# A two-layer block on eight cores: a recurrent scan, token by token, replaced by two sweeps over 32 segments, with gate and routing of the expert layer rewritten

## The chip, the cores and the metric

One Trainium2 chip, all eight NeuronCores, each with its own sequence; nothing is exchanged. The metric is the device time in microseconds (us) of the slowest core. Engines: TensorE (PE; PEld is its weight load), VectorE (DVE), ScalarE (ACT), GpSimd (POOL) and SyncE (SP). SP and POOL issue the DMAs.

## The reference

Per sequence x is 2048 tokens by 1024. What the change touches is layer 0:

```python
def step(state, inp):                      # L0_attn: 128 states
    u_t, sp_t = inp                        # u = x Wi^T + bi, sp = x Ws^T + bs
    state = jnp.tanh(state @ A.T + u_t @ B.T) + sp_t
    y_t = state @ C.T
    return (state, y_t)
...
out = jnp.einsum('bsn,dn->bsd', ys, Wo) + bo
...
x = _layernorm(x + _L0_attn_ref(...))
# L0_ffn: 8 experts of 1024 -> 4096 -> 1024, the best 2 by softmax(x gate_w^T + gate_b)
x = _layernorm(x + _L0_ffn_ref(...))
```

Layer 1 is causal attention of 16 heads with a norm of k and q per head, and a channel mix with a sigmoid gate; both again with residual and layer norm. All inputs and the output are f32.

## The kernel before, in words

The program is recorded by small helpers (`E`, and `DV`, `AC`, `GP`, `MM`, `DMA` for one engine each) into one list per engine, and `realize` writes the lists out; each engine executes its own in order. So the order of the calls is the order on every engine, and nearly every instruction has the same line, L1173; the products of the scan have L1167 (`held_`), the gathers L1158. `w=` names what an instruction waits for. `only_if(flag, tok, name)` puts a block behind a branch that every engine takes or skips after it has waited for `tok`; there is one for an expert with more than CAP = 640 tokens ("x") and two for large layer norm weights ("z", "zz").

*Scan.* A state is tanh + sp, so with C_t = u_t B^T + sp_(t-1) A^T made ahead for 512 tokens in a PSUM bank (`sp_mm`, `sp_ev`, `c_mm`, BWi being Wi and B in one matrix), a token is one product of A with the tanh of the token before, added into its PSUM column, and one tanh of that column:

```python
    for t in range(T):
        if t > 0:
            hold("AT", AT)
            held(ps[:, (t // 512) % 2, t % 512:t % 512 + 1], AT, tanh[:, t - 1:t], (("ac", t),), "sc_p")
...
        E("scalar", "activation", tanh[:, t:t + 1], ps[:, (t // 512) % 2, t % 512:t % 512 + 1], AF.Tanh,
          w=w, s="ac")
        for f in sched.pop(t, ()):
            f()
```

The dictionary `sched`, filled by `at(t, f)`, hangs all other work on a token number: a tile of 128 tokens follows the scan that far behind. Per tile: `tile_state` (stb = tanh + sp), `tile_mm` (stb times WoC, which is C and Wo in one matrix), `tile_xb` (x + bo on POOL), `tile_ln` (residual and layer norm, x1 to DRAM, x1b in bf16), `tile_logit` (eight 1024-wide multiply-and-sum on VectorE, one per expert, with gwr, the gate's rows spread over all partitions), `tile_route` (the best two as one-hot rows, with ties to the lower number), `tile_rank_mm` and `tile_pos` (the row of each token in its expert's list, posU, from running counts) and two indirect DMAs that scatter x1b into xgs. `center` takes the mean off 16 blocks of Wq and Wk and stores them in wcs. W1 of expert 0 is loaded in 16 chunks during the scan, and SP fills xgs with zeros in ten DMAs.

*After the scan.* The overflow flag and the gate values; on SP `load_b2(0)` and `load_xg(0)`, the transposed load of expert 0's rows; on POOL 16 chunks of W2; the branch "x"; then `mlp` for each of eight experts: 512 products of 320 columns (hT = relu(W1 x + b1)) and 320 of 512 columns (yst, to ybs), while POOL loads the next expert's chunks, each 1 MB of f32 in DRAM that lands as 512 KB of bf16, as soon as a chunk's last reader is done. Then the x1 tiles are fetched, the two expert rows of each token gathered with posU and weighted with `gate` (`fetch`, `combine`), and attention and the last block follow.

Of the kernel before, what the change touches and what calls it, by code (L numbers as in the profile page):

```python
# [13 lines left out]
T = 2048  # L14
# [9 lines left out]
LIM = 40.0  # L24

# [4 lines left out]
def build():  # L30
# [9 lines left out]
    xT_d = din("xT", [D, T])  # L40
# [3 lines left out]
    gw_d = din("gw", [NE, D])  # L44
    cf_d = din("cf", [128, 310])
    cb_d = din("cb", [128, 640], BF16)
# [16 lines left out]
    ao_d = scratch("aos", [8, 128, T], BF16)  # L63

# [15 lines left out]
    b2r = [place(f"b2r{i}", [128, D], F32, OB + i * 4096) for i in range(2)]  # L80
# [4 lines left out]
    ohs = [place(f"oh{i}", [128, NTILE, NE], BF16, OM + 2560 + i * 256) for i in range(2)]  # L85
    posU = place("posU", [128, NTILE, 2], U32, OM + 3072)
    MX = place("MX", [128, NTILE], F32, OM + 3200)
    gate = [place(f"gate{i}", [128, NTILE], F32, OM + 3264 + i * 64) for i in range(2)]
    Mcum = [place(f"Mcum{i}", [128, NE], BF16, OM + 3392 + i * 32) for i in range(2)]
    Mt = [place(f"Mt{i}", [128, NE], BF16, OM + 3456 + i * 32) for i in range(2)]  # L90
    flag = place("flag", [128, 2], U32, OM + 3520)
# [11 lines left out]
    xTb = [place(f"xTb{i}", [128, 8, 512], BF16, O2 + i * 8192) for i in range(2)]  # L103
    gwr = place("gwr", [128, NE, D], F32, O2 + 16384)
    bor = place("bor", [128, D], F32, O2 + 49152)
    WoC = place("WoC", [128, D], BF16, O2 + 53248)
    BWi = place("BWi", [128, 8, 128], BF16, O2 + 55296)
    WsB = place("WsB", [128, 8, 128], BF16, O2 + 57344)
    WiN = place("WiN", [128, D], BF16, O2 + 59392)
    WoB = place("WoB", [128, D], BF16, O2 + 61440)  # L110
    AT = place("AT", [128, 128], BF16, O2 + 63488)
    BT = place("BT", [128, 128], BF16, O2 + 63744)
    CN = place("CN", [128, 128], BF16, O2 + 64000)
    bib = place("bib", [128, 512], BF16, O2 + 64256)

    spf = place("spf", [128, T], F32, OH)
    tanh = place("tanh", [128, T], BF16, OH + 8192)
    spb = place("spb", [128, T], BF16, OH + 12288)
    stb = place("stb", [128, T], BF16, OH + 16384)
# [108 lines left out]


    DMA("sync", "lc", cf, cf_d)  # L230
    DMA("sync", "lc", cb, cb_d[:, 0:384])
    t_lc = V("lc")
    DMA("gpsimd", "lw", WiN, WiN_d)
    DMA("gpsimd", "lw", BT, BT_d)
# [78 lines left out]
    for k in range(10):  # L313
        c_mm(0, k)()
# [950 lines left out]
```

How the kernel before makes its waits and increments, by code:

```python
    def run(eng, lst):  # L1144
        for method, args, kw, need, s, n in lst:
            plain = method in HELD or method in ("wait_", "if_", "gather_")
            for sn, v in need if plain else need[:-1]:
                eng.wait_ge(sems[sn], v)
            if method == "wait_":
                continue
            if method == "gather_":
# [4 lines left out]
                        for c in calls:  # L1156
                            call = {k: v for k, v in c.items() if k != "sem"}
                            eng.indirect_dma_start(**call).then_inc(sems[c["sem"][0]], 16)
                continue
# [5 lines left out]
            if method == "held_":  # L1165
                out, weights, rhs = args
                ins = eng.add_instruction(mybir.InstMatmult(
                    name=nc.get_next_instruction_name(), engine=mybir.EngineType.PE, start_tensor_calc=False,
                    stop_tensor_calc=True, tile_size=(128, 128), tile_position=(0, 0), ldweights=False,
                    bass_skip_group_check=True, ins=(eng.lower_ap(rhs), eng.lower_ap(weights)),
                    outs=(eng.lower_ap(out),)))
            else:
                ins = getattr(eng, method)(*args, **kw)
            if need and not plain:
                ins._wait_ge(sems[need[-1][0]], need[-1][1])
            if s is not None:
                ins.then_inc(sems[s], n)
```

## Time and profile before

| | |
|---|---|
| median of 3 runs | 3124.77 us (3118.58 to 3244.63) |
| the profiled execution | 3126.89 us |
| its span, slowest core (core 2) | 3125.2 us |
| spans of the eight cores | 3100.1 to 3125.2 us |
| mean granted TensorE clock | 0.813 |
| busy: PE, PEld, DVE, ACT, POOL | 2225.8, 974.8, 904.7, 1106.0, 480.9 us |
| HBM read, written | 371.72 MB, 69.34 MB |

Busy time is that of one profiled execution; a product's end is modelled, so start-to-start times say more of TensorE than the durations do. "Idle before" of a group is the time its engine stood still just before its instructions, with what ended it. A DMA's time is that from issue to landing. GB/s counts the bytes as they are written: the W chunks are read with twice as many. The clock is the share of 2.4 GHz granted to TensorE.

### The profile page before, as it was taken

The numbers are of one execution on the slowest core, as the hardware profiler recorded it, in microseconds if no ns is written. First come the engines' busy times: TensorE is split into PE (matmuls) and PEld (weight loads), VectorE is DVE, ScalarE is ACT, GpSimd is POOL, SyncE is SP. The second block draws the span as 40 slices with busy tenths as digits, with TensorE's granted clock in tenths as the row PEclk, the third lists the DMA queues.
The fourth block names the chain that finished last, engine by engine and source line by source line (L and its number), as shares of the span: only waits on it lengthen the run. The fifth ranks groups of instructions, "written<-read, shape, count | busy, mean of one in ns | idle before, by whom it ended". The sixth has DMA issues, their size and how long they took to land.

```text
span 3125.2 us, 29218 instructions; the slowest of 8 cores (3100.1 to 3125.2 us)
## 1 busy us (share of the span) xinstructions
PE 2225.8 (71%) x12243; PEld 974.8 (31%) x10294; DVE 904.7 (29%) x1758; ACT 1106.0 (35%) x3045; POOL 480.9 (15%) x503
## 2 busy tenths in 40 slices
PE   2434334333336999999999999956787878848775
PEld 0000000000004564656556465622332323323332
DVE  1334353434432000000000000016643444444454
ACT  1444444444432120302112030204576877823322
POOL 1011010111002021110101011013102323202223
PEclk7555555555557999999999999988998999979888
DMA  9322331111107997979799797536400123151101
GB/s 211 92 69 72 74 78 41 51 41 50 42 24 135 163 166 141 171 141 171 143 159 151 143 169 143 96 122 230 153 8 1 28 44 59 29 117 44 49 27 41
DMA packets 133009, 303.98 MB, mean 97 GB/s; under 512 B 56049, under 2 KB 60530, under 8 KB 130546
## 3 DMA queue, kind: packets, MB, share of 16 engines
q0 software_dynamic: 55152, 174.97, 32.2%
q1 hardware_dynamic: 77698, 126.96, 14.3%
q8 instruction: 92, 1.51, 0.2%
q14 instruction: 67, 0.55, 0.1%
HBM read 371.72 MB, written 69.34 MB: 141 GB/s over the span
## 4 chain that ended last, share of the span: by engine, by line
PE 56%; ACT 20%; issue 11%; DVE 7%; DMA 4%; POOL 3%; POOLq 0%; ACTq 0%; DVEq 0%; SPq 0%
PE ps L1173 45%; ACT tanh L1173 11%; PE ps L1167 11%; ACT PT L1173 4%; ACT rsd L1173 2%; DVE PT L1173 2%; DMA xTb<-xT 2%; POOL x3f L1173 1%; DVE lstf L1173 1%; DVE xk L1173 1%; ACT sq L1173 1%; DMA sumC<-stg 1%; DVE rf L1173 1%; DVE lsmf L1173 1%; POOL yB L1158 1%
## 5 line engine op out<-in xcount | busy, mean ns | idle before, releaser
L1167 PE MATMUL ps<-tanh,AT 128*128 128x1 bf16 x2047 | 336.2, 164 | 513.2 <-ACT tanh L1173 513.1
L1173 PE MATMUL ps<-xgT,W 128*128 128x320 bf16 x4096 | 560.0, 300 | 14.7 <-DMA xgT<-xgs 14.6
L1173 ACT ACTIVATE tanh<-ps 128x1 bf16<-128x1 f32 x2048 | 355.2, 173 | 573.1 <-PE ps L1167 548.6
L1173 PE MATMUL ps<-W,hT 128*128 128x512 bf16 x2560 | 553.8, 379 | 0.0
L1173 ACT ACTIVATE hT<-ps,cf 128x640 bf16<-128x640 f32 x256 | 203.3, 794 | 834.0 <-PE ps L1173 834.0
L1173 PEld LDWEIGHTS ps<-xgT,W 128*128 128x128 bf16 x4096 | 401.4, 98 | 173.0 <-issue 14.7
L1173 DVE TENSOR_TENSOR yst<-ps,b2r 128x1024 f32<-128x1024 f32 x40 | 49.0, 1225 | 1074.7 <-PE ps L1173 1060.2
L1173 PEld LDWEIGHTS ps<-W,hT 128*128 128x128 bf16 x2560 | 250.5, 98 | 300.8
L1173 ACT ACTIVATE PT<-ps 128x1024 bf16<-128x1024 f32 (+7 forms) x384 | 271.7, 791 | 77.9 <-PE ps L1173 74.8
L1173 POOL DMA_DIRECT2D W<-w x256 | 136.6, 539 | 858.2 <-PE ps L1173 798.6
L1173 PE MATMUL ps<-PT,Vg 128*128 128x512 bf16 (+3 forms) x640 | 194.0, 364 | 54.9 <-DVE PT L1173 54.3
L1173 PE MATMUL ps<-qz,KT 128*128 128x512 bf16 (+3 forms) x640 | 189.9, 365 | 16.7 <-POOL qz L1173 12.1
L1173 DVE TENSOR_TENSOR PT<-PT,cb 128x128 bf16<-128x128 bf16 x256 | 109.1, 445 | 174.3 <-ACT PT L1173 171.4
L1173 DVE SCALAR_TENSOR_TENSOR junk<-zt,gwr 128x1024 f32<-128x1024 f32 x128 | 156.6, 1224 | 3.9
L1173 PEld LDWEIGHTS ps<-WoC,stb 128*128 128x128 bf16 x32 | 3.3, 105 | 489.0 <-issue 459.9
L1173 DVE TENSOR_TENSOR stb<-tanh,spf 128x128 bf16<-128x128 bf16 x16 | 4.7, 292 | 388.4 <-ACT tanh L1173 388.4
L1173 PEld LDWEIGHTS ps<-PT,Vg 128*128 128x128 bf16 x640 | 64.7, 101 | 141.3 <-DVE PT L1173 89.9
L1173 PEld LDWEIGHTS ps<-Mt,cb 128*128 128x128 bf16 x16 | 1.7, 103 | 316.3 <-issue 297.2
L1173 POOL TENSOR_TENSOR aoT<-stg,recB 64x2048 bf16<-64x2048 f32 x15 | 67.6, 4505 | 191.2 <-DMA recB<-rcs 191.2
L1173 PE MATMUL ps<-Wu,aoT 128*128 128x512 bf16 x256 | 69.0, 431 | 31.8 <-DVE aoT L1173 21.0
L1173 POOL TENSOR_TENSOR rs<-ve,mhalf 128x1 f32<-128x1 f32 x16 | 9.0, 566 | 528.9 <-DVE ve L1173 528.9
L1173 PE MATMUL ps<-WvS,x2T 128*128 128x512 bf16 x256 | 66.0, 417 | 31.9 <-ACT x2T L1173 31.9
(154 smaller groups left out, 1865.1 us busy)
## 6 DMA issues: line engine op xcount, KB each, us to landing
W<-w POOLq DMA_DIRECT2D x256, 512.0 KB, 35.6
ybs<-yst SPq DMA_DIRECT2D x40, 512.0 KB, 6.8
xgs<-zero SPq DMA_DIRECT2D x10, 1024.0 KB, 37.6
xt<-x SPq DMA_DIRECT2D x16, 512.0 KB, 3.8
x1s<-zt SPq DMA_DIRECT2D x16, 512.0 KB, 2.9
x1c<-x1s SPq DMA_DIRECT2D x16, 512.0 KB, 7.1
x2s<-x1c SPq DMA_DIRECT2D x16, 512.0 KB, 2.8
recB<-rcs SPq DMA_DIRECT2D x16, 512.0 KB, 4.7
```

The source lines that it names most:

```text
L1158: eng.indirect_dma_start(**call).then_inc(sems[c["sem"][0]], 16)
L1167: ins = eng.add_instruction(mybir.InstMatmult(name=nc.get_next_instruction_name(), engine=mybir.EngineType.PE, start_tensor_calc=False, st ...
L1173: ins = getattr(eng, method)(*args, **kw)
```

## The change

The sequence is cut into NSEG = 32 segments of SEG = 64 tokens, and x is handed over so that row 32 s + k is token s of segment k: a tile of 128 rows is four tokens of each segment. Two sweeps of 64 links each go over 32 columns at a time. The first starts every segment from nothing and keeps only its last tanh in e1; the second starts segment k from the end of k - 1 in the first, and its tanh are the result. Then the ends of the two sweeps are compared; if any of the 31 differs by more than TOL = 2^-6, flag column 2 is set, and the branch "s" does the scan again token by token, and all tiles after it.

Tiles, gate and routing are made by `post`. The gate is no longer taken from the normalised x1: with z = x + y, the logits are rs (z gw - mean sum(gw)), where x gw is eight f32 products of 512 columns (`gate_x`), y gw is a product of stb with G3 (the gate times WoC, in three bf16 parts; `gate_y`), and mean and rs are the tile's own. `route` does four tiles at once on 128x32 operands. bo comes in as a product with three bf16 rows, b3. Six tiles (ahead = 6) are hung on links 68, 78, ... 118; ten come after the last link. x transposed is loaded as f32 by SP and cast by VectorE and POOL. Only 4 chunks of W1 can be loaded early, since x tiles lie in the place of the others, and 8 of W2 after the first two gates. The centering moves under the experts, in 32 half blocks. b2r has one buffer. posU and gate are in segment order; posN and gateN, for the gathers, are got by writing both to DRAM and reading them back, and the branch "x" waits for that (t_pos).

```diff
-    xT_d = din("xT", [D, T])
+    xT_d = din("xT", [4, 128, 4096])
...
-            held(ps[:, (t // 512) % 2, t % 512:t % 512 + 1], AT, tanh[:, t - 1:t], (("ac", t),), "sc_p")
...
+    for n in range(128):
+        sweep, s_ = divmod(n, 64)
+        col = (s_ % 16) * NSEG
+        bank = cbank if sweep else (0, 1, 2, 3)
+        o = ps[:, bank[s_ // 16], col:col + NSEG]
+        w = [st[("c2" if sweep else "c1"), s_ // 16]] if s_ % 16 == 0 else []
+        if n > 0:
+            if sweep == 0:
+                rhs = t1[:, (s_ - 1) % 2, :]
+            else:
+                rhs = tanh[:, (s_ - 1) * NSEG:s_ * NSEG] if s_ else e1[:, 0:NSEG]
+            hold("AT", AT)
+            w.append(held(o, AT, rhs, (("ac", n),), "sc_p"))
...
+        t = E("scalar", "activation", dst, o, AF.Tanh, w=w, s="ac")
...
+    for i in range(6):
+        load_x(i)
+    xgz = xg_d[0:MAIN, :].rearrange("(a p r) d -> a p (r d)", p=128, r=2)
+    for i in range(MAIN // 256):
+        DMA("sync", "zf", xgz[i], zero, w=(t_zero,))
...
+        t = DMA("sync", "lb3", bl_d.rearrange("(a r) d -> a r d", a=1), bol, w=(t,))
+        st["b3"] = DMA("sync", "lb3", b3[1:3, :], bl_d, w=(t,))
...
+        def tile_z(i, after):
+            b = 0 if after and i % 2 else 2
+            sl = slice(i * 128, (i + 1) * 128)
+            t = DV("tensor_tensor", stb[:, sl], tanh[:, sl], spf[:, sl], ALU.add, w=(S["h", i], st["spe", 3]))
+            for j in range(2):
+                MM(ps[:, b + j, :], stb[:, sl], WoC[:, j * 512:(j + 1) * 512], start=True, stop=False,
+                   w=(t, st["woc"], S.get(("zf", b)), S["h", 15] if after else None))
+                t2 = MM(ps[:, b + j, :], ones_b[0:3, :], b3[:, j * 512:(j + 1) * 512], start=False, stop=True,
+                        w=(st["b3"], st["b30"]), inc=(j == 1))
...
+        def gate_x(nt):
+            for k in range(8):
+                t = MM(ps[0:8, 4, :], gwT[:, k, :], xTf[nt][:, k, :], start=(k == 0), stop=(k == 7),
+                       w=(S.get(("xf", nt)), S.get("xg"), t_lc, st["sg"], st["spe", 3]), inc=(k == 7))
...
+    t = DV("tensor_tensor", dif[:, 0:NSEG - 1], tanh[:, T - NSEG:T - 1], e1[:, 1:NSEG], ALU.subtract, w=(st["h", 15],))
...
+    for i in range(ahead, NTILE + 1):
+        if i < NTILE:
+            tile_z(i, True)
+        tile_n(i - 1, True)
+        j = i - ahead
+        if j % 2 == 0 and j // 2 < 4:
+            gate_x(j // 2)
+        if i in (7, 9, 11, NTILE):
+            nt = min(j // 2, 3)
+            gate_y(nt)
+            route(nt)
...
+    load_xg(0, w=t_x1all)
+    for c in range(4, 16):
+        load_w1(0, c, w=t_x1all + (t_vscan, t_gscan, tk["xg", 0]) + t_scat)
+    for c in range(8, 16):
+        load_w2(0, c, w=(t_pscan, tk["xg", 0]))
...
-    with only_if(flag[0:1, 0:1], t_fl, "x"):
+    DMA("sync", "pw", po_d.rearrange("(i p) c -> p i c", p=128), posU, w=(t_gate,))
+    DMA("sync", "pw", ga_d.rearrange("(i p) c -> p i c", p=128), gate)
+    t_pw = V("pw")
+    for h in range(2):
+        for d, o in ((po_d, posN), (ga_d, gateN)):
+            DMA("sync", "pr", o[64 * h:64 * h + 64], d.rearrange("(s i h) c -> h s i c", i=NTILE, h=2)[h], w=(t_pw,))
+    t_pos = V("pr")
...
+    with only_if(flag[0:1, 0:1], t_pos, "x"):
```

TensorE in the scan. Before, in the last fifth of the scan, a tile's product with WoC and its rank products (Mt, Mcum) stand between runs of the scan's product with AT:

```order
L1167 MATMUL ps<-tanh,AT 128x1 x2
L1173 MATMUL ps<-WoC,stb 128x512
L1173 LDWEIGHTS AT
L1167 MATMUL ps<-tanh,AT 128x1 x54
L1173 MATMUL ps<-Mt_64,cb 128x8
L1173 MATMUL ps<-Mcum_62,cb 128x8
L1173 LDWEIGHTS AT
L1167 MATMUL ps<-tanh,AT 128x1 x72
L1173 MATMUL ps<-WoC,stb 128x512
```

In the second sweep of the change, links 66 to 70 (xTb is x transposed in bf16, BWi and ps as before, b_110 is b3, cb its column of ones):

```order
L1369 MATMUL ps<-tanh,AT 128x32
L1375 MATMUL ps<-xTb_70,BWi 128x512
L1375 LDWEIGHTS AT
L1369 MATMUL ps<-tanh,AT 128x32 x2
L1375 MATMUL ps<-xTb_70,BWi 128x512
L1375 MATMUL ps<-WoC,stb 128x512
L1375 MATMUL ps<-b_110,cb 128x512
L1375 MATMUL ps<-WoC,stb 128x512
L1375 MATMUL ps<-b_110,cb 128x512
L1375 LDWEIGHTS AT
L1369 MATMUL ps<-tanh,AT 128x32
L1375 MATMUL ps<-xTb_70,BWi 128x512
```

The 72 one-column products between two tiles' work have become ten of 32 columns, and a tile has four products, two of them with b3, ahead of the next link.

SP at the start. Before (bor is bo spread over the partitions, xgs<-zero the zero fill):

```order
L1173 DMA bor<-bo 128x1024
L1173 DMA lnr<-lnrow 1x256
L1173 DMA xt_86<-x 128x1024
L1173 DMA xt_87<-x 128x1024
L1173 DMA gwr<-gw 128x1024 x8
L1173 DMA xgs<-zero 128x4096 x10
L1173 DMA wqf_92<-WqT 128x1024
```

In the change, from the third of the four blocks of x transposed on (xTf, in f32, two DMAs each; xt_73 to xt_78 are the x tiles):

```order
L1375 DMA xTf_67<-xT 128x2048 x2
L1375 DMA xTf_68<-xT 128x2048 x2
L1375 DMA xt_73<-x 128x1024
L1375 DMA xt_74<-x 128x1024
L1375 DMA xt_75<-x 128x1024
L1375 DMA xt_76<-x 128x1024
L1375 DMA xt_77<-x 128x1024
L1375 DMA xt_78<-x 128x1024
L1375 DMA xgs<-zero 128x2048 x20
L1375 DMA bls<-bol 1x2048
L1375 DMA b_110<-bls 2x1024
```

The rows for b3 (bls<-bol out, b_110<-bls back in) stand behind all loads of x and all twenty zero fills.

SP at the end of the scan's stage. Before:

```order
L1173 DMA wcs<-wqc_95 128x1024
L1173 DMA x1s<-zt_89 128x1024
L1173 DMA b2r_50<-b 128x1024
L1173 DMA_TRANSPOSE xgT_46<-xgs 128x8x640
L1161 TENSOR_LOAD flag
L1162 COMPARE_AND_BRANCH
```

In the change, behind the branch "s" (pos and gas are the DRAM copies of posU and gate):

```order
L1350 UNCONDITIONAL_BRANCH
L1375 DMA_TRANSPOSE xgT_46<-xgs 128x8x640
L1375 DMA b2r<-b 128x1024
L1375 DMA pos<-posU 128x16x2
L1375 DMA gas<-gate 128x16x2
L1375 DMA posN<-pos 64x16x2
L1375 DMA gateN<-gas 64x16x2
L1375 DMA posN<-pos 64x16x2
L1375 DMA gateN<-gas 64x16x2
L1363 TENSOR_LOAD flag
L1364 COMPARE_AND_BRANCH
```

Six DMAs have come in between the transposed load of the first expert and the branch that every engine takes.

## Rows read from the trace of the kernel before

**Rows 1.** Windows of the span: busy us of each engine, clock, DMA share, GB/s.
```profile
core 2: us, PE busy (x) PEld busy (x) DVE busy (x) ACT busy (x) POOL busy (x), PEclk, DMA share, GB/s
...
1060.00:1800.00 740.00, 740.00 (x4380) 428.38 (x4378) 34.29 (x28) 127.07 (x160) 92.24 (x175) 1.00 0.89 154
...
60.00:300.00 240.00, 99.89 (x587) 5.47 (x85) 91.87 (x202) 94.00 (x542) 22.75 (x21) 0.50 0.35 93
600.00:900.00 300.00, 118.73 (x728) 2.37 (x39) 130.47 (x289) 122.34 (x706) 29.77 (x22) 0.50 0.13 43
```

**Rows 2.** Groups of instructions by form, whole span: busy us, mean ns, idle before.
```profile
L1173 ACT ACTIVATE tanh<-ps 128x1 bf16<-128x1 f32 x2048 | 355.2, 173 | 573.1 <-PE ps L1167 548.6 <-PE ps L1173 24.5
L1167 PE MATMUL ps<-tanh,AT 128*128 128x1 bf16 x2047 | 336.2, 164 | 513.2 <-ACT tanh L1173 513.1
...
L1173 DVE SCALAR_TENSOR_TENSOR junk<-zt,gwr 128x1024 f32<-128x1024 f32 x128 | 156.6, 1224 | 3.9
...
L1173 ACT ACTIVATE x3b<-x3f,lsmf 128x1024 bf16<-128x1024 f32 x16 | 19.8, 1239 | 62.3 <-DVE lsmf L1173 62.3
```

**Rows 3.** Timeline: the scan's first product, the end of TensorE's wait, the last.
```profile
36.24 0.21 PE L1167 MATMUL ps<-tanh,AT 128*128 128x1 bf16 x1
...
67.94 0.61 PE L1173 MATMUL ps<-xTb,WsB 128*128 128x512 bf16 x1 [21.69 <-DMA xTb<-xT]
...
930.27 0.16 PE L1167 MATMUL ps<-tanh,AT 128*128 128x1 bf16 x1 [0.26 <-ACT tanh L1173]
```

**Rows 4.** Chain that ended last (start us, us, what), then the timeline there.
```profile
953.59 3.75 DMA xgs<-x1b,posU
957.51 7.89 DMA xgT<-xgs
965.64 4.44 PE ps L1173 x16
972.40 1104.75 PE ps L1173 x6624
...
965.64 72.13 PE L1173 MATMUL ps<-xgT,W 128*128 128x320 bf16 x512 [14.60 <-DMA xgT<-xgs]
1037.61 69.23 PE L1173 MATMUL ps<-W,hT 128*128 128x512 bf16 x320
```

**Rows 5.** Windows with the DMA engines full: zero fill and loads; the W stream.
```profile
38.00:90.00 52.00, 16.81 (x88) 2.36 (x36) 2.40 (x11) 11.96 (x69) 2.02 (x2) 0.50 1.06 286
970.00:1040.00 70.00, 69.92 (x509) 49.45 (x508) 0.00 (x0) 26.71 (x33) 12.97 (x25) 1.00 1.06 165
```

**Rows 6.** Timeline of the last tile: engines, start us, us.
```profile
930.68 0.29 DVE L1173 TENSOR_TENSOR stb<-tanh,spf 128x128 bf16<-128x128 bf16 x1 [24.99 <-ACT tanh L1173]
...
931.03 1.04 PE L1173 MATMUL ps<-WoC,stb 128*128 128x512 bf16 x2 [0.59 <-DVE stb L1173]
932.24 1.23 DVE L1173 TENSOR_TENSOR zt<-ps,xt 128x1024 f32<-128x1024 f32 x1 [1.27 <-PE ps L1173]
933.50 1.29 DVE L1173 BATCH_NORM_STATS2 bst<-zt 128x6 f32<-128x512 f32 x2
934.82 0.21 DVE L1173 BATCH_NORM_AGGREGATE mv<-bst 128x2 f32<-128x12 f32 x1
935.06 0.15 DVE L1173 TENSOR_SCALAR ve<-mv 128x1 f32<-128x1 f32 x1
...
935.90 0.81 DVE L1173 TENSOR_SCALAR zt<-zt,mv,rs 128x1024 f32<-128x1024 f32 x1 [0.69 <-POOL rs L1173]
...
936.82 0.69 DVE L1173 CAST x1b<-zt 128x1024 bf16<-128x1024 f32 x1
...
947.55 0.17 DVE L1173 TENSOR_TENSOR LG<-LG,cf 128x8 f32<-128x8 f32 x1
...
951.30 0.17 DVE L1173 CAST posU<-tm 128x2 uint32<-128x2 f32 x1
...
952.26 1.02 POOL L1173 DMA_INDIRECT xgs<-x1b,posU  x1 [16.40 <-DVE ge L1173]
...
953.59 0.98 POOL L1173 DMA_INDIRECT xgs<-x1b,posU  x1 [0.30 <-issue]
```

**Rows 7.** DMA in 958 to 1900 us; the eight transposed loads' time to landing.
```profile
DMA packets 78688, 147.68 MB, mean 157 GB/s; under 512 B 45342, under 2 KB 45342, under 8 KB 78632
...
xgT<-xgs SPq DMA_TRANSPOSE x8, 99.9
...
DMA to landing us min/median/max: 7.9/99.9/110.8
```

**Rows 8.** DMA issues of 2730 to 2790 us, then of the whole span (median us).
```profile
rcs<-rC SPq DMA_DIRECT2D x1, 8.0 KB, 7.7
...
xt<-x SPq DMA_DIRECT2D x16, 512.0 KB, 3.8
x1s<-zt SPq DMA_DIRECT2D x16, 512.0 KB, 2.9
...
sumC<-stg SPq DMA_DIRECT2D x16, 8.0 KB, 2.0
rcs<-rC SPq DMA_DIRECT2D x16, 8.0 KB, 1.4
```

More of the change, by code:

```diff
@@ L131, in build @@
[L131 to L138 removed]
+    xTf = [place(f"xTf{i}", [128, 8, 512], F32, O2 + i * 16384) for i in range(4)]
@@ L308, in c_mm @@
+            if k == last:
+                S[name, nt] = t
         return f
@@ new lines, in build @@
+    load_x, tile_z, tile_n, gate_x, gate_y, route, scatter, ends = post(st, 6)
+    for i in range(6):
[3 more added lines that the diff above has]
+        DMA("sync", "zf", xgz[i], zero, w=(t_zero,))
+    t_zf = V("zf")
+    for c in range(4):
+        at(40 + c, lambda c=c: load_w1(0, c, (t_xf[3, 1],)))
+    ahead = 6
+    for i in range(ahead):
+        at(68 + 10 * i, lambda i=i: tile_z(i, False))
+        if i > 0:
+            at(69 + 10 * i, lambda i=i: tile_n(i - 1, False))
@@ new lines, in build @@
+    for i in routed:
+        scatter(i)
+    ends()
+    with only_if(flag[0:1, 2:3], st["fl3"], "s"):
+        in_array[0] = None
+        S = {}
+        for nt in range(4):
+            for k in range(11 if nt == 0 else 10):
+                c_mm(S, nt, k, nt, "c2")()
+            S["xf", nt] = DMA("sync", "lx", xTf[nt].rearrange("p c t -> p (c t)"), xT_d[nt])
+        t = None
+        for n in range(T):
+            k, s_ = divmod(n, SEG)
+            o = ps[:, s_ // 16, (s_ % 16) * NSEG + k:(s_ % 16) * NSEG + k + 1]
+            w = [] if n else [S["c2", nt] for nt in range(4)]
+            if n > 0:
+                hold("AT", AT)
+                w = [held(o, AT, tanh[:, prev:prev + 1], (t,), "sc_p")]
+            prev = s_ * NSEG + k
+            t = E("scalar", "activation", tanh[:, prev:prev + 1], o, AF.Tanh, w=w, s="ac")
+        for i in range(NTILE):
+            S["h", i] = t
+        load_x, tile_z, tile_n, gate_x, gate_y, route, scatter, ends = post(S, 2)
+        for i in range(2):
+            load_x(i)
+        for nt in range(4):
+            S["xf", nt] = ("~s_lx", 64)
+            for i in range(4 * nt, 4 * nt + 4):
+                tile_z(i, True)
+                tile_n(i, False)
+            gate_x(nt)
+            gate_y(nt)
+            route(nt)
+            for i in range(4 * nt, 4 * nt + 4):
+                scatter(i)
+        ends()
+        for c in range(8):
+            DMA("gpsimd", "w2", W2[:, 2 * c:2 * c + 2].rearrange("p k o -> p (k o)"), w2_d[0, c], w=(V("p"),))
+        in_array[0] = None
```

619 lines of the change are left out of this document (349 added, 270 removed).

## The prediction

> **What bounds the kernel now.** I read the windows first. From 60 to 900 us TensorE, VectorE and ScalarE are each busy about 40% of the time at a granted clock of 0.50, and the DMA share falls to 0.13; from 1060 us TensorE is busy without a gap at 1.00 [rows 1]. A stretch in which three engines idle that much is a chain of short links. The groups of instructions name it: 2,048 tanh of one column (173 ns) wait 548.6 us for 2,047 one-column products (164 ns), which wait 513.1 us for the tanh [rows 2]. The second link runs at 36.24 us and the last at 930.27: 894.0 us, less the 21.7 us in which TensorE waits for the second block of x (until 67.94 us), over 2,046 steps is 0.426 us a token [rows 3]. The chain that ended last says what follows: the last scatter (953.59), 7.89 us for the transposed load of the first expert's rows, the first expert product at 965.64, then products [rows 4]. So **the first 965.64 us are the scan and its tail**, and 3126.89 - 965.64 = 2161.25 us are experts, attention and the last block.
>
> **What is taken away.** The 2,048 links become 128: two sweeps of 64, each over 32 columns, one token of each segment. 31 more columns cost under 0.05 us a link (the two link operations have 173 and 164 ns for one column; a 128x512 product takes 0.216 us at the fast clock, 69.23 us over 320 [rows 4], so 0.43 at this one, and 32 columns 0.03), so a link is about 0.45 us, the pure chain 58 us. The 128 gate operations on VectorE (1,224 ns each, [rows 2]) go; they lay beside the scan, except for the last tile's eight. What was hidden behind 2,048 links now stands in the open: that is the real price.
>
> **The new head, step by step.**
> (a) SP issues in order 8 loads of x transposed (1 MB each), 6 of x, 20 zero fills of xgs (512 KB each), and only then the two small copies that bring bo's low parts into b3: 8.4 + 3.1 + 10.5 = 22.0 MB in one queue. POOL adds 4 chunks of W1 and the small weights, about 6 MB read. Between 38 and 90 us the same sort of mix moved 286 GB/s at a DMA share of 1.06 [rows 5]. 28 MB at that rate are 98 us. Every tile's product into the residual stream needs b3, and the first of them stands in TensorE's row at link 68, so the scan, which would be there at about 60 us, waits to **98 us**. Bounds: the 22 MB alone, 77 us; 28 MB at a fifth less than that rate, 122 us.
> (b) Six tiles are done inside the second sweep, one every ten links. VectorE per tile: 0.29 + 1.23 + 1.29 + 0.21 + 0.15 + 0.81 + 0.69 = 4.7 us [rows 6]; it waits inside the tile for four products (1.04 us for two [rows 6], so 1.9 with the start), and 0.5 of gaps: 7.1 us. Ten links with their fillers take 10 x 0.45 + 1.9 = 6.4, so VectorE paces. 98 + 5 x 7.1 + 1.9 + 9 x 0.45 = **140 us**. The branch's flag (five short operations and a product round trip) is 1.5 us.
> (c) Ten tiles and four routings follow with no scan to hide them. A tile here leaves its normalising to ScalarE (two of 1.24 us [rows 2], beside VectorE): 0.29 + 1.9 + 1.23 + 1.29 + 0.21 + 0.15 + 0.16 is 5.3. A routing is 35 small operations; the old ones took 947.55 to 951.30 for 24, 0.16 each, and with four times the columns I take 0.19: 7 us. TensorE executes in order, so the f32 gate product (8 products of 512 columns, G us) stands between a pair's two tile products; VectorE can cover 3 us of it. A pair with its routing is 0.3 + 1.9 + G + 1.9 + 3.3 + 7 = 14.4 + G, three times; the last part is one pair without routing, two tiles and a routing, 25 + G. Sum 68 + 4G. G is not in this trace: below, eight bf16 products at 0.43, 3.4 us; above, four products of bf16 halves for each f32 one at the slow clock, 13.8 us. I take 9.5, between the fast clock's 6.9 and the slow end, because gaps lie between: 106 us, bounds 82 and 123. **247.5 us**.
> (d) When the last routing ends, six tiles are still to be scattered: 12 indirect DMAs, 1.3 us apart (952.26 to 953.59), then 3.8 to land: 19.4. Before, it was two. Then 7.9 for the transposed load: **274.8 us**.
> (e) The new wait. The segment order has to be turned into the natural one, so posU and gate go to DRAM and back, and *every engine* waits for that at the overflow branch, TensorE ahead of its first expert product. Each of the six copies is cut into 8-byte records: 2 x 2,048 out, 4 x 1,024 in. On SP they stand behind the transposed load; and when that lands, POOL starts 20 chunks of W (12 of W1, 8 of W2). A chunk is 0.524 MB at 165 GB/s [rows 5], 3.18 us: 63.5 us of full DMA engines. The trace has a twin: the transposed load, 5,120 records of 256 bytes (eight of them make 40,960 of the 45,342 packets under 512 B [rows 7]), lands in 7.9 us alone and in 99.9 beside the W stream [rows 7]. At 99.9/5120 us a record 3,254 of the 4,096 outgoing ones pass in 63.5 us; the other 842 and the 4,096 incoming ones at 7.9/5120 take 1.3 + 6.3; two landings of 2.0 [rows 8]: **75 us**. Low end: all at the rate of the lone load, 2 x (6.3 + 2.0) = 17 us. High end, from the 128 records of rcs<-rC, 1.4 us alone and 7.7 beside a weight load [rows 8]: 49 ns a record in the stream, 1,290 records; the other 6,900 at 11 ns, 76 us; with landings 143.
> The first expert product then starts at 275 + 75 + 1 for the branch, less rounding: **about 350 us** instead of 965.6.
>
> **What a page says of (e).** The row shows 99.9 us against 7.9 for the same copy [rows 7]. The Trainium skill, "DMA: Bandwidth & Descriptors", section "Queues, rings and completion order", says that an engine changes between queue rows only at packet borders and drains some 9 to 17 descriptors of one queue first. By that rule 256 records per engine would be about 20 packets and pass quickly, which is the first rival's time; the 99.9 us speak against it.
>
> **What a page says of (c).** "FP8 and Floating Point Precision", section "TensorE Precision Notes", of the Trainium skill gives four passes for a true f32 product. No run here shows it; by it G would be 6.9 to 13.8 us and the sum would stay where it is.
>
> **The rest.** The experts keep their products. W1 chunks 0 to 3 and W2 0 to 7 come early, the rest during (e), so TensorE finds them there; afterwards a chunk costs 3.18 us of DMA and 4.5 of TensorE (71.97 us over 16, [rows 4]), as before. The 32 half-size centering steps move under the experts, where VectorE is idle but for five operations an expert; b2r has one buffer, but 69 us between its reader and its next one. Two x1 fetches a tile instead of one add 0.4 us of SP. Cost: 0, and if a cover failed a few us. 350 + 2161.25 = 2511 us against the profiled execution's 3126.89, which is 2.1 above the median of 3124.77: **2509 us**.
>
> **Rivals.**
> *The records pass* (0.20): (e) is 17 us, and the first expert product is at 292. 2509 - 58 = 2451. For it: 64 KB in all. Against: [rows 7, 8]. TensorE then starts while chunks still arrive at 3.18 us against a need of 4.5: no stall.
> *The scan isn't held by b3* (0.10): if 20 zero fills are faster than I count, link 68 comes at 60, and the price of (a) goes: 2509 - 38 = 2471.
> *The records are slower than the twin* (0.11): 8-byte writes at the rate of rcs<-rC. 2509 + 68 = 2577.
> *The ends differ and the branch is taken* (0.03): the sweeps start each segment from a guess. If on any core a state at a segment's end moves by more than 2^-6 = 0.0156 between sweeps, all is done again token by token: 41 products (18), 2,048 x 0.426 = 872, sixteen tiles with only two buffers, whose store (2.9) and load (3.8 [rows 8]) stand in the loop, some 8 us each, 128, four gates and routings 66, eight reloads of W2 25: 1,109 us more, 3618 us, slower than before by 16%. It decides at that one comparison. Against it: the two sweeps worked out in numpy from the reference's inputs, with a rounding to bf16 after each tanh, leave at most 0.0064 on all eight sequences.
>
> **Chances.** The forecast has 0.56, the rivals 0.20, 0.10, 0.11 and 0.03. The range 2425 to 2580 takes in each of the first three, the records' bounds and those of (c), not the two fast rivals together (2413). No change can be told from less than 2% here (62 us), and nothing in the sum lies near 3125: faster 0.96, same 0.01, slower 0.03.
>
> **What would show it.** Right: TensorE's first expert product near 350 us, at once after a wait on the copies of pos and gas; 1,024-column tile operations of VectorE from about 98 us with the tanh of links 69 on behind them; copies of pos landing 60 us and more after issue; no gap of TensorE in the experts. (a) is wrong if b3 lands before 75 us, (e) if posN lands within 20 us of xgT, (c) if the last posU is written before 215 or after 270 us. The whole is wrong if any one-column tanh appears.

## The result: 2677.78 us in the profiled execution, 0.858 of the time before

In some executions the cores of one die, or of both, ran slower at a lower granted clock; these are left out of every time and ratio below. The changed kernel is faster by 14.2%: ratio 0.8579, 95% interval 0.8542 to 0.8617, from two executions of each kernel. They took 2677.78 us, the profiled one, with a span of 2676.2 on its slowest core, and 2678.65. The forecast was 2509 us with a range of 2425 to 2580, so the sign was right, but the forecast was 169 us too low, far outside the range.

Where the 169 us lie is seen with three marks: the first expert product, the last y addition of the experts, and the end.

| us | before | forecast | after | e8 (below) |
|---|---|---|---|---|
| first expert product | 965.6 | 350 | 365.5 | 364.3 |
| from there to the end of the last y addition | 1112.9 | as before | 1270.6 | 1112.9 |
| from there to the end of the span | 1046.7 | as before | 1040.1 | 1056.4 |

The marks are those of the slowest core of each profiled execution. On all eight cores the experts (second row) took 1112.4 to 1113.2 us before and 1250.3 to 1270.6 after; in e8 1112.7 to 1113.3 on seven cores and 1127.4 on the eighth. The third row differs by up to 24 us between the cores of one execution (1033.2 to 1051.2 after), so differences of that size in it say nothing of an edit.

The head, to which nearly all of the forecast's working went, is 15 us off. The experts, to which it gave two sentences and the cost 0, are 158 us off.

**The head.** These are pieces of the chain that ended last (start, us, what), from the start of the kernel to the first expert product, to be read against [rows 4]:

```profile
78.38 10.94 DMA bls<-bol
89.38 2.52 DMA b<-bls
91.95 1.67 PE ps L1375 x3
...
134.07 11.71 PE ps L1375 x24
...
242.81 2.85 DMA xgs<-x1b,posU
...
255.98 6.29 SPq L1375
263.40 10.52 SPq L1375
273.92 71.19 another core or an unknown queue
346.81 9.35 SPq L1375
356.20 4.69 DMA gateN<-gas
360.89 4.62 issue
365.51 54.61 PE ps L1375 x381
```

The chain runs through the small copies of b3, as step (a) said: issued at 78.38 us behind the zero fills, landed at 91.9. Then come the tiles, the scatters, the transposed load, and the long stretch from 263.40 to 345: that is the copy of gate to DRAM, which the chain can't name. Two products of TensorE mark the end of the scan, and one the f32 gate product:

```profile
131.77 0.18 PE L1369 MATMUL ps<-tanh,AT 128*128 128x32 bf16 x1 [0.29 <-ACT tanh L1375]
133.16 0.19 PE L1375 MATMUL ps<-fl,cb 128*128 128x1 bf16 x1 [1.20 <-DVE fl L1375]
...
136.20 8.29 PE L1375 MATMUL ps<-xTf,cg 128*8 128x512 f32 x16
```

The DMA issues (KB each, median us from issue to landing) give the price of the new copies and one surprise, AT:

```profile
xgs<-zero SPq DMA_DIRECT2D x20, 512.0 KB, 14.2
AT<-AT POOLq DMA_DIRECT2D x1, 32.0 KB, 38.7
posN<-pos SPq DMA_DIRECT2D x2, 8.0 KB, 13.2
gateN<-gas SPq DMA_DIRECT2D x2, 8.0 KB, 9.0
pos<-posU SPq DMA_DIRECT2D x1, 16.0 KB, 15.0
gas<-gate SPq DMA_DIRECT2D x1, 16.0 KB, 81.7
```

The 81.7 us are not the price of each record. The first copy, pos, landed in 15.0 us, as the W stream began. The profile counts what each queue moved. From 285 to 345 us, and then from 355 to 362 us (packets, MB, busy share; the software queue carries the W stream, the hardware queue SP's records):

```profile
q0 software_dynamic: 1952, 7.11, 100.4%
q1 hardware_dynamic: 1909, 0.02, 4.1%
...
q1 hardware_dynamic: 3933, 0.03, 32.6%
q0 software_dynamic: 126, 0.43, 34.4%
```

While the stream runs, one 8-byte record of gas passes for each piece of the stream (4 KB, but for its small completion marks). When the stream is through, some 3,900 records of the copies back pass in 7 us. So a record beside the stream costs a turn as long as a 4 KB piece, and the last copies back wait for the stream's end.

**The experts.** Windows, one per expert; the first, the second and the last of eight. The six between 502 and 1495 us take 163 to 169 each:

```profile
core 4: us, PE busy (x) PEld busy (x) DVE busy (x) ACT busy (x) POOL busy (x), PEclk, DMA share, GB/s
365.50:502.00 136.50, 136.49 (x810) 80.15 (x811) 11.10 (x16) 26.75 (x33) 13.24 (x25) 0.98 0.58 104
502.00:671.00 169.00, 143.74 (x847) 83.17 (x845) 12.14 (x17) 25.46 (x32) 18.58 (x36) 0.92 0.79 138
...
1495.00:1634.80 139.80, 139.75 (x838) 81.69 (x835) 12.32 (x17) 25.43 (x32) 2.46 (x4) 1.00 0.48 100
```

TensorE lacks 22 to 27 us in each of the six, 145.4 us in all. Its mean granted clock in them is 0.92 to 0.93 instead of 1.00. The products themselves take some 2 us more in each: 157.7 us lost in the table, less 145.4 of waiting, are 12.3 over six experts. The groups of instructions (busy, mean ns | idle before, releaser) say who was late, and for what that engine waited:

```profile
L1375 PE MATMUL ps<-W,hT 128*128 128x512 bf16 x2560 | 566.0, 384 | 145.4 <-DVE yst L1375 145.4
...
L1375 DVE TENSOR_REDUCE wsum<-wqf 128x8 f32<-128x512 f32 x32 | 21.9, 686 | 874.3 <-DMA wqf<-WqT 496.6
```

TensorE waits for the y addition. VectorE, busy for 12 us of 165, stands in a centering step waiting for its piece of WqT. The chain of waits inside the second expert shows who holds that piece:

```profile
507.09 1.24 DVE yst L1375
508.39 0.32 SPq L1375
508.80 96.52 SPq L1375
605.37 5.39 DMA wqf<-WqT
...
628.15 1.23 DVE yst L1375
629.42 43.73 PE ps L1375 x192
```

and SP's own timeline names the piece of 96.52 us:

```profile
508.80 96.52 SPq L1375 DMA_TRANSPOSE xgT<-xgs  x1
605.37 0.57 SPq L1375 DMA_DIRECT2D wqf<-WqT  x1
606.00 0.69 SPq L1375 DMA_DIRECT2D b2r<-b  x1
```

The whole mechanism is in these lines. SP issues the transposed load of the next expert's rows at an expert's start, and the issue itself holds SP for 96.5 us while the W stream runs. Behind it stands the first centering load. VectorE, in order, stands in the first centering step; the two y additions stand behind four such steps, and TensorE, with two pairs of PSUM banks, can't begin its third W2 tile. The first expert is a control that the trace holds by itself: there SP took 7.76 us for the same load (364.70), no stream ran beside it, and TensorE had no gap.

The load also takes turns with the stream: from 530 to 600 us the stream's queue moved 3,049 packets and SP's, which carried the transposed load alone, 3,051, of 256 bytes. Its issue ended at 605.3 us, and by 608 the stream was through.

### The profile page after: what moved, and what is told of

Read it like the earlier page. It is cut to its first block, busy times and chain, and to the rows that moved or that the text cites. A ratio compares the mean times of both kernels' runs of the same rounds, so it can differ in the third digit from the quotient of the medians.

```text
span 2676.2 us, 25572 instructions; the slowest of 8 cores (2645.0 to 2676.2 us)
## 1 busy us (share of the span) xinstructions
PE 1995.4 (75%) x10556; PEld 996.3 (37%) x10515; DVE 689.0 (26%) x1344; ACT 806.8 (30%) x1151; POOL 441.0 (16%) x487
## 4 chain that ended last, share of the span: by engine, by line
PE 33%; SPq 26%; DVE 11%; ACT 10%; issue 9%; DMA 5%; POOL 3%; another core or an unknown queue 3%; POOLq 0%; DVEq 0%; ACTq 0%
PE ps L1375 33%; SPq L1375 26%; ACT PT L1375 5%; ACT rsd L1375 2%; DVE PT L1375 2%; DMA wqf<-WkT 2%; DMA wqf<-WqT 2%; POOL x3f L1375 1%; DVE lstf L1375 1%; DVE xk L1375 1%; ACT sq L1375 1%; DVE wsum L1375 1%; DMA sumC<-stg 1%; DVE rf L1375 1%
## 5 line engine op out<-in xcount | busy, mean ns | idle before, releaser
L1375 PE MATMUL ps<-W,hT 128*128 128x512 bf16 x2560 | 566.0, 384 | 145.4 <-DVE yst L1375 145.4
L1375 DVE TENSOR_REDUCE wsum<-wqf 128x8 f32<-128x512 f32 x32 | 21.9, 686 | 874.3 <-DMA wqf<-WqT 496.6
L1375 PEld LDWEIGHTS ps<-qz,KT 128*128 128x128 bf16 x640 | 50.2, 99 | 107.2 <-ACT PT L1375 76.7
L1375 PE MATMUL ps<-xk,Wkf 128*128 128x512 bf16 x256 | 63.2, 410 | 14.0 <-DVE xk L1375 14.0
L1375 PE MATMUL ps<-Wr,xr 128*128 128x512 bf16 x256 | 57.9, 379 | 14.1 <-DVE xr L1375 8.7
L1375 PE MATMUL ps<-x2T,WqS 128*128 128x512 bf16 x256 | 65.1, 391 | 0.0
L1375 PE MATMUL ps<-x2T,WkS 128*128 128x512 bf16 x256 | 60.6, 379 | 0.0
L1375 POOL TENSOR_TENSOR x3f<-x3f,rf 128x1024 f32<-128x1024 f32 x16 | 37.5, 2342 | 140.6 <-DVE rf L1375 140.6
## 6 DMA issues: line engine op xcount, KB each, us to landing
xgs<-zero SPq DMA_DIRECT2D x20, 512.0 KB, 14.2
```

The source lines that it names most:

```text
L1375: ins = getattr(eng, method)(*args, **kw)
```

## The experiments

All kernels are the changed one with edits. Times are medians, of two executions for e2, e3, e4 and e10, of one for e6, and of three or four for the others, "first" is the first expert product, "y" the start of the last y addition.

**e1: centering ahead of the transposed load.**

```diff
     for e in range(NE):
+        for q in range(4):
+            center_load(4 * e + q)
+            center_run(4 * e + q)
         if e + 1 < NE:
             load_xg(e + 1, ...)
...
-            if ev == "m1" and j % 8 == 0: center_load(...)
-            if ev == "m1" and j % 8 == 4: center_run(...)
```

> The four centering steps of an expert are put ahead of the next expert's transposed load on SP, and nothing else is changed. Theory 1 (order on SP: a centering load stands behind a transposed load whose issue holds SP for 94 us; VectorE stands in the centering step, the yst additions behind it, and TensorE waits for a PSUM bank): the six waits of some 25 us before the products ps<-W,hT go, experts 1 to 6 take 138 to 142 us instead of 163 to 169, and the time falls by 135 to 155 us, to about 2530 us. Rival (the added DMA traffic and VectorE work of the centering slow the experts wherever they stand): the experts stay above 155 us and the time above 2620 us. Risk for theory 1: the transposed load now holds SP over the first yst store, which may cost up to 10 us an expert.

Measured: 2635.12 us (lowest 2629.41), ratio 0.8425 (0.8398 to 0.8452), 43 us below the changed kernel. Theory 1's 2530 is missed by 105 us; the rival's time came true (above 2620), but not its experts above 155 us: the transposed loads of experts 2 to 7 follow each other in 150 to 154 us. Of the 145.4 us of TensorE's wait for yst 66.5 stayed; the experts took 1214.0 us instead of 1270.6, and the first product came 7 us later. VectorE's waits name the new holder (us, times, longest), and SP's and TensorE's timelines the place:

```profile
DVE yst L1374 <- DMA b2r<-b: 274.5, 6, 46.8
```
```profile
597.41 39.80 SPq L1374 DMA_TRANSPOSE xgT<-xgs  x1
637.27 0.57 SPq L1374 DMA_DIRECT2D b2r<-b  x1
```
```profile
642.83 43.07 PE L1374 MATMUL ps<-W,hT 128*128 128x512 bf16 x192 [10.67 <-DVE yst L1374]
```

The small load of b2 now stood behind the same issue. A step takes 15 us here (with the W stream beside it, against 5 between the steps of the kernel without the edit), so four of them are 60. With the steps out of the way about half of the wait for yst was gone (78.9 of 145.4 us); the thing they shared with b2 is what stood ahead of them in SP's order.

**e8: e1, and b2's load ahead of everything in the expert.**

```diff
     for e in range(NE):
+        if e > 0:
+            load_b2(e, w=(tk["yv", e - 1],))
         for q in range(4):
...
-            if ev == "m1" and j == 1 and e > 0:
-                load_b2(e, w=(tk["yv", e - 1],))
```

> e1_center_first, and the load of b2 moved from behind the transposed load to the expert's start. Theory A (what was left of the stall in e1 was the y addition's wait for b2, 274 us in all on VectorE, 11 us an expert on TensorE): the stall goes, 60 to 75 us below e1, 2560 to 2580 us, and experts 1 to 6 take 138 to 142 us. Theory B (the y stores, which also stand behind the transposed load, end the wait instead): yst waits for ybs or the experts stay near 150 us, and the gain is under 20 us.

Measured: 2535.33 us, ratio 0.8121 (0.8098 to 0.8145), 100 below e1, more than I expected: beside the 66.5 us of waits for yst, e1 had a gap of 18.8 us in its first expert, and its products took 16 us more in all. The trace names no releaser for that gap. It ends at 450.08 us, 2.4 behind the start of a 16 KB load on the profile's instruction queue; gaps at the same place in e5 and e11 end 2.6 and 2.3 behind such a load. That TensorE waited for it is likely and not shown. The groups show TensorE without any wait for yst, and the window over all experts is to the tenth that of before (1112.90 us):

```profile
L1374 PE MATMUL ps<-W,hT 128*128 128x512 bf16 x2560 | 553.8, 379 | 0.0
```
```profile
364.30:1477.20 1112.90, 1111.15 (x6656) 651.85 (x6656) 98.62 (x136) 204.47 (x257) 120.39 (x226) 1.00 0.83 150
```

All 32 centering steps are in that window. Their work costs nothing; the order of the transposed load, the steps and b2 in SP's queue cost 157.7 us on the slowest core, and 138 to 158 on the eight.

**e5: the transposed load later, the steps where they were.**

```diff
     for e in range(NE):
-        if e + 1 < NE:
-            load_xg(e + 1, w=(tk.get(("m1", e - 1, 31)),))
...
+            if ev == "m1" and j == 31 and e + 1 < NE:
+                load_xg(e + 1, w=(tk.get(("m1", e - 1, 31)),))
```

> One edit on the changed kernel: the transposed load of expert e+1 is issued after the 32nd first product of expert e instead of at the expert's start; the four centering steps stay where they are. Theory A (SyncE's order is the cause): at the expert's start the centering load no longer stands behind the transposed load's 94 us issue, VectorE is free for the y additions, and the transposed load finds the weight stream idle, as it did in the kernel with the centering first (issue 41 us instead of 94). It runs from 72 to some 115 us of an expert that lasts 137, so the third y addition (110 us) waits a few us at most: experts 1 to 6 take 138 to 142 us instead of 163 to 169, the wait of TensorE for yst falls from 145 to under 25 us, and the time is 2510 to 2550 us. Theory B (the load is slow wherever it stands, 94 us): it lands 166 us after the expert's start, the next expert waits 30 us for xgT, and the time is 2690 to 2720 us.

Measured: 2540.33 us (lowest 2533.26), ratio 0.8124 (0.8096 to 0.8152); no wait for yst. Theory A. The edit adds no wait, it only puts the load behind the four steps and b2 in SP's order, which is nearly the order of e8; the two agree within 0.3%. SP's timeline in the second expert:

```profile
584.36 40.29 SPq L1375 DMA_TRANSPOSE xgT<-xgs  x1
624.76 24.93 SPq L1375 DMA_DIRECT2D ybs<-yst  x4
```

The issue takes 40 us here and 96 in the kernel without the edit, but it ends at much the same point: 101 us after the y addition that closes the expert before (at 524), against 98 there (at 507). That is how long the stream lasts: 16 chunks of W2 are issued in the 14 us ahead of that addition and 16 of W1 behind the products that follow, and the stream's queue is through by 623 us here and by 608 in the kernel without the edit, within 3 us of the end of the issue in both. A transposed load started at the head of this stream stands in it to its end; started 74 us behind its first chunk, the load stands for the rest, and is through before the third y addition. One edit of two lines gives back 138 us.

**e2 and e4: two ways to shorten the new wait, without the repair.** e2 issues the last 12 chunks of W1 and 8 of W2 behind the copies of positions and gates:

```diff
     t_pos = V("pr")
+    for c in range(4, 16):
+        load_w1(0, c, w=t_x1all + (t_vscan, t_gscan, tk["xg", 0], t_pos) + t_scat)
+    for c in range(8, 16):
+        load_w2(0, c, w=(t_pscan, tk["xg", 0]))
```

> The last 12 W1 and 8 W2 chunks of expert 0 are issued only when the copies of pos and gas are back, so that the records move alone. Theory 1 (the 8-byte records are slow because the W stream takes turns with them on the DMA engines): from the landing of xgT to the first expert product it takes 25 to 40 us instead of 98, the first product comes near 305 us instead of 365.5, the chunks arrive faster (3.2 us) than TensorE takes them (4.5), and the time falls by 50 to 65 us, to about 2620 us. Rival (8-byte records are slow by themselves, or the branch costs tens of us): the first product stays after 345 us and the time gets no shorter.

e4 lets the overflow branch wait for the flag alone:

```diff
-    with only_if(flag[0:1, 0:1], t_pos, "x"):
+    with only_if(flag[0:1, 0:1], t_fl, "x"):
...
-                          w=(..., t_pscan, t_pos))
+                          w=(..., t_pscan, t_ascan))
```

> The overflow branch waits for its own flag, as before the change, and not for the copies of pos and gas; only the gathers wait for these. Theory 1 (that wait costs the span from the landing of xgT to 365 us): the first expert product comes within 8 us of xgT's landing, near 275 us; expert 0's products then run beside both the W stream and the records, and if chunks keep arriving in 3.2 us the time falls by 85 to 95 us, to about 2588 us; if the records slow the stream, TensorE waits in expert 0 and 20 to 50 us of that are given back. Rival (the branch or the chunks and not the copies hold TensorE): the first product stays after 340 us.

Measured: e2 2666.47 us (0.8527, 0.8508 to 0.8545), e4 2681.29 (0.8574, 0.8553 to 0.8596). Both did what they were to do at the start, and both handed it back inside the first expert. TensorE in e2, then in e4 (start, us):

```profile
306.52 72.41 PE L1375 MATMUL ps<-xgT,W 128*128 128x320 bf16 x512 [66.84 <-issue]
...
444.79 43.36 PE L1375 MATMUL ps<-W,hT 128*128 128x512 bf16 x192 [38.24 <-DVE yst L1375]
```
```profile
273.15 72.59 PE L1375 MATMUL ps<-xgT,W 128*128 128x320 bf16 x512 [32.62 <-DMA xgT<-xgs]
...
453.65 43.03 PE L1375 MATMUL ps<-W,hT 128*128 128x512 bf16 x192 [70.24 <-DVE yst L1375]
```

The first product came 59 and 92 us earlier. But in e2 the second transposed load (306.41, 96.86 us on SP) now meets the stream that had been over before; in e4 SP stands in the copies back until 411.8. In both the first centering load is late and the y additions with it. My expectations left out SP's order once more, the very step that had failed in the prediction. Both had forecast 50 to 95 us; neither time can be told from the changed kernel's, whose interval theirs overlap.

**e6: e5 and e2 together.**

> The transposed load moved as in e5_xg_late, and the weight chunks behind the copies of positions and gates as in e2_w_after_pos. Theory A (e2's gain of 59 us at the start was handed back behind the transposed load of expert 1, whose issue took 97 us and held the centering step, and TensorE waited 38 us for yst in expert 0): with that load out of the way the gain stays, 45 to 60 us below e5_xg_late, some 2460 to 2490 us. Theory B (the later weight chunks are what costs: TensorE waits for W in expert 0): the gain over e5 is under 20 us and the trace shows TensorE waiting for W.

Measured: 2460.32 us, from one execution, so no ratio is given; first at 302.0, y at 1413.9, no wait for yst and none for W. Span against span (2458.7 and 2542.9) that is 84 us below e5: first comes 62 earlier, and 18 more lie in the experts, where e5 had a gap of 16 in the first one. That is more than theory A's 45 to 60, in part because e5's slowest core had the slowest experts: 1131.2 us, where the eight cores took from 1112.3 up. The stream, moved away from the copies, costs TensorE nothing: theory A.

**e3, e7, e9: the loads of the head.** e3 puts the 20 zero fills behind b3's copies:

```diff
+    def zero_fill():
         for i in range(MAIN // 256):
             DMA("sync", "zf", xgz[i], zero, w=(t_zero,))
-    t_zf = V("zf")
+    at(3, zero_fill)
+    t_zf = ("zf", 16 * (MAIN // 256))
```

> The twenty zero fills of xgs are issued behind the two copies for b3 instead of ahead of them. Theory 1 (b3, last in SP's queue, holds the first tile's product and with it the scan at link 68, but only from about 82 to 92 us, since a late load of AT had already put the scan's start off to 48.6 us): b3 lands before 70 us, the wait goes, the last link ends at about 120 us instead of 131.9, the time falls by 8 to 14 us, to about 2667 us. Rival (as predicted, the zero fill holds the scan by some 38 us): it falls by more than 25 us. Rival 2 (VectorE's tiles pace the sweep anyway): no change within 4 us.

Measured: 2697.49 us, 0.8626 (0.8607 to 0.8644). None of the three forecasts came true. The edit worked at its place: bls was issued at 54.86 us instead of 78.38, the end-of-scan flag product came at 124.60 instead of 133.16. But the first expert product stayed (365.1), because gas landed at 343 us as in the kernel without the edit (345), though the first W chunk was issued 4.5 us earlier. So the head was not shorter. Of the 20 us of span above the kernel without the edit, 14 lie behind the last y addition, where nothing was changed, and 7 in the experts. That last stretch took 1041.3 to 1054.2 us on the eight cores here and 1033.2 to 1051.2 in the kernel without the edit, so the 14 us are of the size by which cores differ and don't show an effect of the edit. The intervals of the two ratios overlap.

e7 is e6, with the later quarters of xT waiting for WsB and AT:

```diff
-                              xT_d[nt, :, 2048 * h:2048 * h + 2048])
+                              xT_d[nt, :, 2048 * h:2048 * h + 2048], w=(t_lw2,) if nt else ())
```

> e6_late_wpos, and the loads of the three later quarters of xT wait until WsB and AT are there. Theory A (AT, 38.7 us from issue to landing behind 4 MB of xT, holds the first link of the scan at 48.6 us): AT lands by 20 us, the first link starts near 22 to 26 us, and the kernel ends 15 to 25 us before e6. Theory B (a later load of the flag's or of b3's copies, or the xT quarters, which now arrive 10 us later, hold the links or the first tiles): the first link is early but the last link stays near 131 us, and the gain is under 6 us.

Measured: 2467.45 us (lowest 2461.27, against e6's 2460.32), ratio 0.7908 (0.7869 to 0.7947); no gain. Theory B. In TensorE's timeline of e7 the first products of the state start as soon as AT is there, at 19 us instead of 41 in e6, and then:

```profile
18.97 3.24 PE L1375 MATMUL ps<-xTb,WsB 128*128 128x512 bf16 x8 [4.99 <-DMA AT<-AT]
...
95.47 0.60 PE L1375 MATMUL ps<-b,cb 3*128 3x512 bf16 x1 [29.28 <-DMA b<-bls]
```

Two loads hold the scan in turn. Without the first, b3 holds it; that is step (a) of the prediction in its pure form. e9 takes both away (e7 and e3 together):

> e7_late_wpos_at, and the 20 zero fills behind b3's copies as in e3_zero_last. Theory A (two loads hold the head in turn: with AT early the first link starts at 28 us instead of 47, but TensorE then waits 29.3 us for b3, whose copies stand behind the zero fills until 94 us; either edit alone is taken up by the other): both together bring the last link from 131 us to 105 to 112 us, the first expert product from 302 us to 278 to 286 us, and the time 15 to 25 us below e7, 2437 to 2447 us. Theory B (the scan is held by the tiles' vector work or by the x loads, not by loads at the head): within 6 us of e7.

Measured: 2445.27 us (2442.66 to 2452.21), ratio 0.7824 (0.7804 to 0.7845), 22 below e7. The flag's product comes at 107.23 us instead of 136.69 and the first expert product at 274.47 instead of 302.23. Theory A, at its upper end.

**e10: e9 with the branch on the flag (e4's edit).**

> e9_at_zero, and the overflow branch waits for the flag alone and the centering loads for it too, as in e4_branch_flag. The weight chunks still wait for the copies. Theory A (the first product no longer waits for the copies, 30 us, but the fifth weight chunk is issued only when they have landed, so TensorE waits for W about 15 to 20 us in expert 0): 8 to 18 us below e9. Theory B (expert 0 runs at the pace of the chunks until they are in, 48 us from issue to landing at the median): no gain, within 5 us of e9.

Measured: 2444.92 and 2446.07 us against e9's 2445.27: no gain, theory B's number. TensorE's timeline shows three waits in place of one:

```profile
246.29 20.32 PE L1378 MATMUL ps<-xgT,W 128*128 128x320 bf16 x128 [32.22 <-DMA xgT<-xgs]
279.26 53.99 PE L1378 MATMUL ps<-xgT,W 128*128 128x320 bf16 x384 [12.65 <-DMA W<-w]
...
402.99 16.93 PE L1378 MATMUL ps<-W,hT 128*128 128x512 bf16 x64 [13.92 <-DVE yst L1378]
```

28 us earlier, then 12.65 for the chunks, as theory A had it, and 13.92 more at the third y tile, behind a transposed load that took SP 72.8 us: neither theory had that one. Expert 0 had no slack to give.

**e11: e5, positions and gates as records of 16 bytes in one tensor.**

```diff
-    DMA("sync", "pw", po_d..., posU, w=(t_gate,))
-    DMA("sync", "pw", ga_d..., gate)
+    DMA("sync", "pw", pg_d..., pgU, w=(t_gate,))
...
-        for d, o in ((po_d, posN), (ga_d, gateN)):
+        for d, o in ((pg_d, pgN),):
```

> e5_xg_late, with positions and gates side by side in one tile and one DRAM tensor: one copy out of 2048 records of 16 bytes instead of two of 2048 records of 8 bytes each, and two copies back instead of four, all beside the weight stream as before. Theory A (each record pays a turn against the chunks, whatever its size: 4096 records took 82 us): half the records take some 40 us, the first expert product comes at 315 to 330 us instead of 364, and the time is 35 to 50 us below e5, 2490 to 2508 us. Theory B (the copy waits for the queued chunks to drain, not by records): the gas copy lands near 345 us as before and the time is within 10 us of e5.

Measured: 2520.26 us (2515.31 to 2522.66), ratio 0.8058 (0.8039 to 0.8076), 20 below e5. SP's timeline:

```profile
263.59 0.42 SPq L1373 DMA_DIRECT2D pgs<-pgU  x1
276.07 1.40 SPq L1373 DMA_DIRECT2D pgN<-pgs  x2
337.87 0.37 SPq L1373 DMA_DIRECT2D wqf<-WqT  x1
```

The first expert product came at 338.03 us. By the time it lies between the theories, but theory A's mechanism is what the queues show: from 280 to 330 us SP's queue moved 2,075 packets beside the stream's 2,199, one for one. The forecast counted the wrong records. In e5 the 2,048 of pos had passed as the stream began and most of those coming back passed behind it; beside it went the 2,048 of gas and a few hundred. Here the 2,048 outgoing ones pass as it begins, in 12.4 us, and the 2,048 coming back beside it. So nearly as many take turns with the stream as before, and the wait falls from 100 us to 74 and not to half. It is the records that meet the stream that are dear.

**e12: e9 and e11's records.**

> All edits that helped, together: e9_at_zero with the packed records of e11. With the weight chunks waiting for the copies, the copies run alone; in e9 they take from 239 us to the first product at 274.5 us. If half the records halve that (25 us to land outwards, 8 back), the first product comes at 260 us and the time is 10 to 16 us below e9, 2428 to 2436 us. If their time alone is latency and the rest of the queue, the gain is under 5 us.

Measured: 2423.79 us (2423.28 to 2424.69), ratio 0.7770 (0.7756 to 0.7784), 21 below e9, more than the 10 to 16 expected; first at 258.37, y at 1370.2. The first product comes 16 us earlier, which is the gain of the records themselves. It is the fastest kernel of the study, 254 us below the changed kernel's profiled execution.

## Why the prediction was wrong

**The step that failed is "The rest"**: "The 32 half-size centering steps move under the experts, where VectorE is idle but for five operations an expert ... Cost: 0, and if a cover failed a few us." Measured, 157.7 us on the profiled core. The idle share of VectorE was the wrong thing to look at. A centering step is a load on SP, three operations on VectorE and a store on SP, and the load stands behind an instruction that holds SP for 94 to 97 us. The row was there: the transposed loads land after a median of 99.9 us [rows 7], and in the same trace their issue holds SP for a median of 93.9 us. I used it for the price of a record in (e) and didn't ask what is queued behind such a load in the loop. "b2r has one buffer, but 69 us between its reader and its next one" counts products and not SP's order: b2's load stands behind the same issue. In the changed kernel the centering's wait covered that, and e1 brought it out. e8 is the proof: all steps done, the order alone changed, 1112.9 us again.

**(a)** "98 us": the pieces of the chain give 91.9. The mechanism was right (e7: 29.3 us of waiting for b3 once AT is out of the way; e3: bls 23.5 us earlier). What I missed is that the scan would not have been at link 68 by 60 us anyway, because AT, a copy of 32 KB, took 38.7 us behind the xT loads. The rival "scan isn't held by b3" would therefore have got much less than its 38 us: e3 brought the scan's end forward by 8.6.

**(b)** 140 us forecast, 131.8 measured; the tiles run six to seven us apart where 7.1 was forecast (91.95, then 97.99, 104.40, 111.41, 118.41).

**(c)** 106 us forecast; from the last link (131.8) to the last posU (238.0) are 106. The gate product G was put at 9.5 and is 8.3 to 9.5 us; the mean granted clock was 0.79 to 0.87 in the windows of the first three. At 0.87 eight products took 8.29 us, 1.04 each. A bf16 product of that size at the full clock is 0.216 (the prediction's 69.23 us over 320), so an estimated 0.25 at 0.87, and the f32 one is 4.2 of them. The Trainium skill, "FP8 and Floating Point Precision", section "TensorE Precision Notes", gives four passes for a true f32 product, and the trace agrees. My value between the two clocks was good because the mean clock lay between them.

**(d)** 27.3 forecast for scatters and transposed load, 29.6 measured, to the first chunk behind it at 267.65. The 12 indirect DMAs are 1.28 us apart.

**(e)** 75 us forecast from landing to landing; 93.2 measured (267.65 to 360.89), and 4.6 to the first product. From the transposed load's landing the copies out took 77.5 us where I had 67, the copies back 15.7 where I had 8. The sizing by the twin was 20% low, in the direction of the third rival, and that it came so near is in part luck. It had 3,254 of the outgoing records beside the stream, at 19.5 ns each. In fact the 2,048 of pos passed as the stream began, and the 2,048 of gas took turns with its 4 KB pieces, one for one, at some 31 ns each (60 us over 1,909). Without the stream beside it the copy of gas landed in 24.7 us (e9) instead of 81.7.

The prediction's paragraph on the page for (e) drew the wrong conclusion. The Trainium skill, "DMA: Bandwidth & Descriptors", section "Queues, rings and completion order", says that a DMA engine goes round the queue rows that have work and drains one packet, some 9 to 17 descriptors, from each before it changes. That doesn't make a short queue pass quickly: each of its packets waits for one of the stream's, whose pieces are 4 KB. The trace agrees with the taking of turns (1,909 to 1,952); how many descriptors make a turn no run here shows. So the 99.9 us spoke against my reading of the page, not against the page.

So the terms of the head sum to 365.5 - 350 = +15.5 us, the experts to +157.7, and what follows them is 6.6 shorter than before: 167 of the 169 us; the last 2.1 is the forecast's step from the profiled execution to the median. The 6.6 are within what cores differ by. None of the four rivals named the failing place.

## What to carry to other kernels

When work is moved "under" a busy engine, go through every queue that the work passes, not through the engine that computes it: write down what stands ahead of its load and what stands behind its wait, with the duration of the issue, not only of the transfer. An instruction that holds its queue for 95 us belongs behind all short loads whose readers are needed sooner, and into a stretch in which the stream rests. And measure an improvement only after the next holder is out of the way: e2, e4, e3 and e7 gave at most 12 us, while e2's edit was worth over 70 us in e6 (one execution), and e3's with e7's 22 in e9.

## What the hardware did that I had not expected

- The issue of a transposed load holds SP as long as the load is slowed. In the changed kernel it took 6.3 and 7.8 us with no stream beside it and 94 to 97 started 14 us behind the stream's first chunk. In e1 and e5 to e12 it took 36 to 46 us from the second expert on (in the second it started 73 to 79 us behind that chunk), and 64 to 73 in the first expert of e6, e7, e9, e10 and e12. What stands behind it on SP starts only then. The DMA share was 1.06 from 510 to 605 us, while it stood. Beside the stream its pieces pass one for one with those of the stream.
- A small copy on POOL's software queue, issued at 3.74 us, landed 38.7 us later beside SP's loads (272 GB/s over the first 50 us); with six of these held back it was there at 19 us.
- Centering steps one behind another take 5 us each late in the expert and 15 us at its start, with the stream beside them.
- The gaps of 22 to 27 us cost more than themselves: in those experts the mean granted clock was 0.92 to 0.93 and the same products took some 2 us more.

Left open: what TensorE waited for in the gap of 10 to 19 us in the first expert of e1, e5 and e11, and whether a gate product of bf16 parts would shorten the tiles after the scan, which wasn't tried.
